# RWKV-style scan on one core: k, w and r in another channel order, v copied once a batch into its own tile, two working tiles instead of four

## The reference, cut to what matters

```python
xk, xw, xv, xr, xg = ...            # five learned mixes of x and x shifted by one position
w = exp(-exp(time_decay + tanh(xw @ td_w1) @ td_w2))   # (b, l, h, s), h = 32 heads, s = 16
r, k, v = xr @ Wr.T, xk @ Wk.T, xv @ Wv.T              # the same shape
def step(s, rkvw):                  # for each head a 16 x 16 state, s[i, j]
    a = k_t[..., :, None] * v_t[..., None, :]
    out = einsum('bhi,bhij->bhj', r_t, u * a + s)
    s = a + w_t[..., :, None] * s
    return s, out
out = scan(step, s0, (r, k, v, w))  # 128 steps
og = groupnorm(out) * gn_w + gn_b
x1 = x + og * silu(xg @ Wg.T) @ Wo.T
...                                 # a feed-forward part with three 512 x 512 products
...                                 # attention over ctx: scores, softmax, product, output
```

## Time and profile before

| | |
|---|---|
| median of 3 runs | 1021.33 us (1015.73, 1021.33, 1030.74) |
| profiled execution | 1016.36 us, its span 1014.6 us |
| busy: PE, DVE, POOL, ACT | 896.1, 691.5, 536.5, 396.5 us |
| mean granted TensorE clock | 0.936 of full |
| DMA | 150.69 MB, of which 64 v copies of 1 MB |
| first and last chunk | POOL starts at 112.8 us, PE has read the last at 777.6 us |

### The profile page before, as it was taken

How to read it: one execution, slowest core, us unless ns; L and a number is a source line. 1 busy time by engine, 2 the same in 40 slices (tenths; PEclk the granted TensorE clock), 3 DMA queues, 4 the chain that set the end, 5 groups by cost and what they waited for, 6 DMA issues and landing times.

```text
span 1014.6 us, 10745 instructions
## 1 busy us (share of the span) xinstructions
PE 896.1 (88%) x3588; PEld 398.5 (39%) x3588; DVE 691.5 (68%) x907; ACT 396.5 (39%) x819; POOL 536.5 (53%) x573
## 2 busy tenths in 40 slices
PE   1679978799786899688998999899998999979998
PEld 1233433343322343243343444344443454444454
DVE  6234499789988687888887698988998224442342
ACT  2013412333212241133223254565355554465395
POOL 2000388669987749648886778889682101000010
PEclk9687997899977899698999999999999999999999
DMA  7351679969689877878979844779642022001001
GB/s 270 134 125 73 179 178 222 233 171 233 162 187 216 209 184 196 212 145 224 243 182 281 216 112 100 183 192 227 163 99 83 21 73 83 21 4 39 21 0 42
DMA packets 100089, 150.69 MB, mean 149 GB/s; under 512 B 22850, under 2 KB 64066, under 8 KB 91842
## 3 DMA queue, kind: packets, MB, share of 16 engines
q1 hardware_dynamic: 73410, 129.03, 50.4%
q10 hardware_dynamic: 26624, 20.98, 8.5%
HBM read 115.38 MB, written 33.55 MB: 147 GB/s over the span
## 4 chain that ended last, share of the span: by engine, by line
PE 59%; DVE 14%; POOL 12%; issue 6%; ACT 5%; ACTq 2%; DMA 2%; SPq 0%; POOLq 0%; DVEq 0%
PE PS L1318 38%; PE PS L1381 4%; PE PS L1543 4%; POOL VB L704 4%; PE PS L1440 3%; PE PS L1520 2%; DVE PS L1033 2%; PE PS L1325 2%; POOL VB L699 2%; DVE VB L1150 2%; DVE M L1030 2%; DVE VB L1030 2%; POOL VB L695 2%; DVE M L1033 2%; PE PS L1454 1%
## 5 line engine op out<-in xcount | busy, mean ns | idle before, releaser
L1318 PE MATMUL PS<-M,W 128*128 128x512 f32 x672 | 329.8, 634 | 23.7 <-DVE M L1033 12.3
L1318 PEld LDWEIGHTS PS<-M,W 128*128 128x128 f32 x672 | 128.7, 202 | 198.2 <-issue 167.5
L704 POOL TENSOR_TENSOR VB<-VB 128x1024 f32<-128x1024 f32 x64 | 151.4, 2366 | 58.9 <-ACT VB L849 56.2
L1150 DVE TENSOR_TENSOR_SCAN VB<-PS,VB 128x512 f32<-128x512 f32 x128 | 149.1, 1206 | 25.9 <-POOL VB L704 17.3
L587 POOL TENSOR_SCALAR NM<-MV 128x2 f32<-128x2 f32 (+1 forms) x24 | 6.2, 258 | 283.7 <-DVE MV L1278 183.0
L1030 DVE TENSOR_TENSOR VB<-VB,PS 128x2048 f32<-128x2048 f32 x64 | 145.9, 2280 | 1.5
L695 POOL TENSOR_TENSOR VB<-KR,VB 128x1008 f32<-128x1008 f32 x64 | 129.7, 2026 | 17.5 <-DMA VB<-scr_vs 17.5
L699 POOL TENSOR_TENSOR VB<-WG,VB 128x1008 f32<-128x1008 f32 x64 | 129.3, 2020 | 0.0
L1033 DVE SCALAR_TENSOR_TENSOR PS<-PS,VEC,SX 128x512 f32<-128x512 f32 x80 | 60.2, 752 | 87.7 <-PE PS L1381 72.4
L1318 PE MATMUL PS<-W,M 128*128 128x512 f32 x224 | 105.1, 595 | 0.0
L1296 DVE TENSOR_REDUCE SM<-PS 128x1 f32<-128x512 f32 x64 | 44.0, 688 | 58.9 <-PE PS L1543 58.4
(11 more groups left out here) (167 smaller groups left out, 1280.5 us busy)
## 6 DMA issues: line engine op xcount, KB each, us to landing
VB<-scr_vs SPq DMA_DIRECT2D x64, 1024.0 KB, 7.9
W<-in_w SPq DMA_DIRECT2D x8, 1024.0 KB, 9.8
X<-in_x SPq DMA_DIRECT2D x4, 1024.0 KB, 8.2
scr_vs<-STG ACTq DMA_DIRECT2D x64, 64.0 KB, 5.7
scr_v<-STG ACTq DMA_DIRECT2D x16, 256.0 KB, 6.9
scr_w<-STG ACTq DMA_DIRECT2D x16, 256.0 KB, 8.3
scr_k<-STG ACTq DMA_DIRECT2D x16, 256.0 KB, 2.7
KR<-scr_k SPq DMA_DIRECT2D x16, 256.0 KB, 8.1
```

The source lines that it names most:

```text
L704: po.tensor_tensor(flat(bv[:, 0]), flat(bv[:, 0]), flat(bv[:, 1]), ALU.add).then_inc(g_kv, 1)
L1150: sc = dv.tensor_tensor_scan(s_, PS[:, 5, :], b_, 0.0, ALU.mult, ALU.add)
L1318: mm = pe.matmul(o, l, r, start=i == 0, stop=i == 3)
```

## The change

- **Order of k, w, r.** The host orders k, w, r, the decay, the initial state and `u` by `turn` like v: chunk m now has rows m, m+4, m+8 and m+12 of all 32 heads (partition = 32 x one of the four rows + head). HEAD is filled accordingly; its shape and the matmuls that use it stay.
- **One v copy a batch.** All four chunks of a batch need the same v layout now (32 heads, 4 times over), so v comes in by one copy of 1 MB per batch instead of four: 16 copies instead of 64.
- **Tiles.** VB keeps its four tiles. Two (2 and 3) hold v of a batch, in turn; two (0 and 1) are the working tiles of the chunks (`NB = 2`). The v copy waits for POOL's last operation on the batch two before (`g_kv`). POOL reads v there and writes the working tile, so that POOL's first product of chunk k waits for PE to have read chunk k-2.
- **Initial state.** ACT's copy of zeros is gone; POOL's add runs over columns 1 to 63 of 16 rows (1,008) and no longer waits for ACT; DVE's scan waits for the remaining ACT copy; ACT's copy waits for PE's chunk k-2.
- **Tables.** All five ORDER tables are new.

```diff
-NB = 4
+NB = 2
...
-    "a:23 l:1 a:1 l:1 a:2 p:2 a:1 p:11 a:1 p:3 a:5 p:1 a:1 p:1 a:1 p:3 a:1 p:16 a:1 p:4 a:1 p:9 a:11 p:1 "
+    "a:26 l:2 p:6 a:1 p:7 a:1 p:3 a:5 p:1 a:1 p:1 a:1 p:8 a:1 p:6 a:1 p:7 a:1 p:5 a:8 p:1 a:4 p:1 a:4 "
...
-        VB = sb("VB", [P, NB, 2, S, N2])
+        VB = sb("VB", [P, 4, 2, S, N2])
...
-                    for m in range(C4):
-                        k = C4 * bb + m
-                        if k >= NB:
-                            w.wait_ge(p_scan, k - NB + 1)
-                        for c in range(C4):
-                            w.wait_ge(d_vs[c], 64 * (q + 1))
-                        w.wait_ge(d_s0, 32)
-                        src = vs_rows[q, bb % QB, 8 * m:8 * m + 8].unsqueeze(0).to_broadcast([S, 8, S * L])
-                        sp.dma_start(VB[:, k % NB].rearrange("p s j n -> p (s j n)"), src).then_inc(d_vb[k % NB], 16)
-                        yield
-                        if m == 0:
...
+                    if bb >= 2:
+                        w.wait_ge(g_kv, 12 * (bb - 1))
+                    for c in range(C4):
+                        w.wait_ge(d_vs[c], 64 * (q + 1))
+                    w.wait_ge(d_s0, 32)
+                    src = vs_rows[q, bb % QB].unsqueeze(0).to_broadcast([4, H, S * L])
+                    sp.dma_start(VB[:, 2 + s].rearrange("p s j n -> p (s j n)"), src).then_inc(d_vb[s], 16)
+                    yield
...
-                    w.wait_ge(d_vb[k % NB], 16 * (k // NB + 1))
+                    w.wait_ge(d_vb[s], 16 * (bb // 2 + 1))
+                    if k >= NB:
+                        w.wait_ge(p_scan, k - NB + 1)
                     vo, ve = bv[:, 0, :, 1:N2], bv[:, 1, :, 1:N2]
-                    po.tensor_tensor(vo, KO[:, 0:N2 - 1].unsqueeze(1).to_broadcast([P, S, N2 - 1]), vo,
-                                     ALU.mult).then_inc(g_kv, 1)
+                    po.tensor_tensor(vo, KO[:, 0:N2 - 1].unsqueeze(1).to_broadcast([P, S, N2 - 1]),
+                                     VB[:, 2 + s, 0, :, 1:N2], ALU.mult).then_inc(g_kv, 1)
...
                     w.wait_ge(g_kv, 3 * k + 2)
-                    w.wait_ge(a_s0, 2 * k + 2)
-                    po.tensor_tensor(flat(bv[:, 0]), flat(bv[:, 0]), flat(bv[:, 1]), ALU.add).then_inc(g_kv, 1)
+                    po.tensor_tensor(vo, vo, ve, ALU.add).then_inc(g_kv, 1)
...
-                    w.wait_ge(d_vb[k % NB], 16 * (k // NB + 1))
+                    if k >= NB:
+                        w.wait_ge(p_scan, k - NB + 1)
                     w.wait_ge(v_hd, C4 + 2)
                     ac.activation(VB[:, k % NB, 0, :, 0], S0[:, k, :], ACT.Copy).then_inc(a_s0, 1)
-                    yield
-                    ac.activation(VB[:, k % NB, 1, :, 0], S0[:, k, :], ACT.Copy, scale=0.0).then_inc(a_s0, 1)
                     yield
...
                     w.wait_ge(g_kv, 3 * (k + 1))
+                    w.wait_ge(a_s0, k + 1)
...
-    w8 = [heads(p0("Wk")).T, turn(p0("Wv")).T, heads(p0("Wr")).T, turn(p0("Wg")).T, turn(p0("Wo").T)]
+    w8 = [turn(p0("Wk")).T, turn(p0("Wv")).T, turn(p0("Wr")).T, turn(p0("Wg")).T, turn(p0("Wo").T)]
```

More of the change, by code:

```diff
@@ L317, in rwkv_attention_kernel @@
         d_vs = [sem(f"d_vs{i}") for i in range(4)]
-        d_vb = [sem(f"d_vb{i}") for i in range(NB)]
+        d_vb = [sem(f"d_vb{i}") for i in range(2)]
         d_st_ = {n: [sem(f"d_scr_{n}{m}") for m in range(4)] for n in NAMES}
@@ L490, in stream_load @@
                     yield
-                    for m in range(C4):
-                        k = C4 * bb + m
-                        if k >= NB:
-                            w.wait_ge(p_scan, k - NB + 1)
-                        for c in range(C4):
-                            w.wait_ge(d_vs[c], 64 * (q + 1))
-                        w.wait_ge(d_s0, 32)
-                        src = vs_rows[q, bb % QB, 8 * m:8 * m + 8].unsqueeze(0).to_broadcast([S, 8, S * L])
-                        sp.dma_start(VB[:, k % NB].rearrange("p s j n -> p (s j n)"), src).then_inc(d_vb[k % NB], 16)
-                        yield
-                        if m == 0:
-                            for ready in stored("r", q):
-                                w.wait_ge(*ready)
-                            if bb >= 2:
-                                w.wait_ge(p_end, 3 * bb - 4)
-                            sp.dma_start(KR[:, s, 1], of_batch("r", bb)).then_inc(d_rg[s], 16)
-                            yield
+                    if bb >= 2:
[6 more added lines that the diff above has]
+                    yield
+                    for ready in stored("r", q):
+                        w.wait_ge(*ready)
+                    if bb >= 2:
+                        w.wait_ge(p_end, 3 * bb - 4)
+                    sp.dma_start(KR[:, s, 1], of_batch("r", bb)).then_inc(d_rg[s], 16)
+                    yield
                     for ready in stored("v", q):
@@ L692, in stream_scan @@
                         yield
-                    w.wait_ge(d_vb[k % NB], 16 * (k // NB + 1))
+                    w.wait_ge(d_vb[s], 16 * (bb // 2 + 1))
+                    if k >= NB:
+                        w.wait_ge(p_scan, k - NB + 1)
                     vo, ve = bv[:, 0, :, 1:N2], bv[:, 1, :, 1:N2]
-                    po.tensor_tensor(vo, KO[:, 0:N2 - 1].unsqueeze(1).to_broadcast([P, S, N2 - 1]), vo,
-                                     ALU.mult).then_inc(g_kv, 1)
+                    po.tensor_tensor(vo, KO[:, 0:N2 - 1].unsqueeze(1).to_broadcast([P, S, N2 - 1]),
+                                     VB[:, 2 + s, 0, :, 1:N2], ALU.mult).then_inc(g_kv, 1)
                     yield
                     w.wait_ge(g_wp, 2 * (bb + 1))
-                    po.tensor_tensor(ve, KE[:, 0:N2 - 1].unsqueeze(1).to_broadcast([P, S, N2 - 1]), ve,
-                                     ALU.mult).then_inc(g_kv, 1)
+                    po.tensor_tensor(ve, KE[:, 0:N2 - 1].unsqueeze(1).to_broadcast([P, S, N2 - 1]),
+                                     VB[:, 2 + s, 1, :, 1:N2], ALU.mult).then_inc(g_kv, 1)
                     yield
                     w.wait_ge(g_kv, 3 * k + 2)
-                    w.wait_ge(a_s0, 2 * k + 2)
-                    po.tensor_tensor(flat(bv[:, 0]), flat(bv[:, 0]), flat(bv[:, 1]), ALU.add).then_inc(g_kv, 1)
+                    po.tensor_tensor(vo, vo, ve, ALU.add).then_inc(g_kv, 1)
                     yield
@@ L1178, in stream_end @@
                     w.wait_ge(g_sel, 1)
-                    dv.tensor_reduce(HEAD[:, m, 0, 8 * m:8 * m + 8], ID[:].rearrange("p (i h) -> p h i", h=8), AX_X,
+                    dv.tensor_reduce(HEAD[:, m, 0], ID[:].rearrange("p (g h) -> p h g", h=H), AX_X,
                                      ALU.add).then_inc(v_hd, 1)
@@ L1588, in layout @@
     a = {k: np.asarray(v) for k, v in inp.items()}
-    heads = lambda w: w.reshape(C4, 8, S, -1).transpose(0, 2, 1, 3).reshape(E, -1)
     turn = lambda w: w.reshape(H, 4, 4, -1).transpose(2, 1, 0, 3).reshape(E, -1)
@@ L1602, in layout @@
     vec += [cols(p0("maa_stack")[0, f]) for f in MIXES]
-    vec += [cols(heads(p0("time_decay"))[:, 0])] + [cols(turn(p0(n))[:, 0]) for n in ("gn_w", "gn_b")]
+    vec += [cols(turn(p0("time_decay"))[:, 0])] + [cols(turn(p0(n))[:, 0]) for n in ("gn_w", "gn_b")]
     vec += [cols(p0(n)) for n in ("ln2_w", "ln2_b", "ffn_maa_k", "ffn_maa_r")]
@@ L1618, in layout @@
         "td1": chunks(p0("td_w1")),
-        "td2": np.concatenate([heads(p0("td_w2").T).T] * 2),
+        "td2": np.concatenate([turn(p0("td_w2").T).T] * 2),
         "wl1": np.stack([odd(p1("Wn").T), p1("Wm").T, p1("Wl"), odd(p1("Wo")).T], axis=1),
@@ L1622, in layout @@
         "st01": ctx[:, 0:2, :].reshape(B, 2, C4, P).transpose(3, 2, 1, 0),
-        "s0": ctx[:, 2:2 + S, :].reshape(B, C4, 8, S, S).transpose(3, 2, 0, 1, 4).reshape(P, B * C4, S),
-        "u": heads(p0("u").reshape(E)).reshape(C4, P).T,
+        "s0": ctx[:, 2:2 + S, :].reshape(B, H, 4, 4, S).transpose(2, 1, 0, 3, 4).reshape(P, B * C4, S),
+        "u": turn(p0("u").reshape(E)).reshape(C4, P).T,
     }
```

## The result

The changed kernel takes **1060.3 us** (median of 4, 1056.82 to 1064.16), the kernel before 1020.3 beside it: ratio **1.0378** [1.0289, 1.0467], slower. The forecast was 1009, its range ended at 1046, and "slower" had a chance of 0.22. The profiled execution took 1064.16 us, its span is 1062.4.

The account below looks back on a forecast made before the run. PE was nearly full everywhere, with the chunks at times setting the pace, 54 us at most. From 1016.4, -24 for POOL's waits and +12 for two tiles gave 1004 profiled; from 1021.3, 1009 us; range 978 to 1046.

Parts of the forecast that it names:

- slower: Whole kernel: the outcome beyond the measurable 2%, above 1042 us; chance 0.22.
- Hidden: SP queue: the v copy has about one batch, 41 us, against a landing of 7.9, so it costs 0.
- The landing of 7.9 us: v copies: time to landing, read from the trace before and used for the new copy, 7.9 us.
- four engines: Rival, v copies: a leading broadcast of 4 keeps each copy to four DMA engines, landing 31.6 us; 1047 us, chance 0.12.
- The rival's price, 38 us,: Four engines, v copies: 14 us for the first batch plus 24 for transfers SP issues behind a copy; 1009 to 1047.
- -24 us for POOL's waits: POOL beside the chunks: its waits for ACT and the copies, 73.7 us, go; -24 us, bounds 0 and -54.
- The share rule: POOL: 45% of what makes it late goes, so 45% of the chunks' 54 us is won, -24 us.
- +12 for two tiles: Working tiles: POOL's product of chunk k waits for PE's chunk k-2; +12 us, between 0 and 161.
- tiles decide: Rival, working tiles: chunks still taking 22.5 us make two tiles set the pace; 1062 us, chance 0.14.
- the 40 allowed: POOL: sign of a right forecast, a new wait for PE L1440 of under 40 us in all.
- 0 for the 48 copies that go: DMA beside the chunks: 48 copies of 1 MB fewer; 0 beside what is counted elsewhere, bound -20 us.
- 0 for the matmuls moved ahead: PE behind the last chunk: 28 matmuls fewer, 25 us, only cover for a later last chunk; 0.

Follow-up runs that it names:

- 16-engine version: The changed kernel with each batch's v copy issued as four transfers of 32 partitions, each over all 16 DMA engines: 992.5 us, ratio 0.9768 to the kernel before.
- The ACT part alone: The kernel before with only POOL's add over 1,008 columns without waiting for ACT, and ACT's zero copy gone: 1033.6 us, ratio 1.0171.
- the clash removed: The kernel before with POOL's add freed of ACT, plus two waits keeping POOL's products off DVE's M<-SX,VEC,EXT operations: 1018.5 us, ratio 0.9987.

## Why the prediction was wrong, point by point

- **"Hidden": 41 us of cover against a landing of 7.9.** This step failed, and both of its numbers were wrong. The 41 us were the pace of the chunks, as if SP issued the copy the moment its tile was free. SP's wait for PE was removed, but others took its place (L516 217.8 us, L510 173.7), and the copy stands behind them. The cover was 20 us in the median, so a landing of 19 to 24 us was late, and POOL waited for it at eight batches of 16. Of the two numbers the landing decided: the 16-engine version has no more cover and is 68 us faster. The tables with the queue's order were at hand; that the cover ends where the queue's own waits begin could be seen in them.
- **The landing of 7.9 us** was taken from a copy of another shape. Issued the new way it is 21.2 in the median. The chance of 0.12 for "four engines" was too small: the mechanism stood in a rule, the diff had exactly the shape, and nothing in the trace spoke against it. The Trainium skill, "DMA: Bandwidth & Descriptors", section "Rules for kernel authors", has the slowest dimension set the number of engines. Here the trace agrees: four late events a copy where there were sixteen, and 21.2 us with 4 in front for 7.9 with 16 in front, so 2.7 times, not four.
- **The rival's price, 38 us,** was too low against 68. Its first part (14 for the first batch) measured 4 at most. What was missed is that it strikes in later batches too, and about half of it strikes others: the load of r, the stores of g. The rival named LT<-LE as the victim; that one stayed at 2.0 us in the median, with one of 16 at 20.0.
- **-24 us for POOL's waits** failed as well. The ACT part alone brought +15, and 0 with the clash removed. The share rule (45% of 54 us) took a freed engine for a faster kernel. POOL's waits moved to the next one in its order.
- **+12 for two tiles.** A third tile gained nothing, so there is no sign of this cost; all four were not tried. The mean time of a chunk, from its first product to its last matmul, came out at 19.7 us for the forecast 18.9: the working was sound, and "tiles decide" didn't happen, though POOL's wait for PE (77.9) was twice the 40 allowed. The wait was slack.
- **0 for the 48 copies that go:** right for their bytes, to 0.2%.
- **0 for the matmuls moved ahead** was the other failure, with the opposite sign. 25 us were counted as cover for late chunks, and no more. But PE bounds the stretch behind the last chunk (busy 195 of 203 us, before 224 of 237), so work that leaves it is time won if the chunks keep their pace: 34 us there, of which 15 went in later chunks. With the copy repaired the change is worth 24 us (1016.5 to 992.5), more than the forecast's 12. PE's idle time in 161:778 is 45.1 us there, before 60.7, which fits with more work beside the chunks. So the table speaks for the order and not for POOL's waits; but the order by itself was not run, and this stays argued.

## What to carry to other kernels

Before counting the bytes of a transfer, look at its first dimension: a copy of 1 MB with 4 in front took 21.2 us where one with 16 in front took 7.9, and it delayed loads and stores issued behind it. Read a transfer's cover from the issuing queue's order and waits, not from when its tile comes free. And when an engine is freed, look at what it will run beside: an operation that comes earlier can land on a neighbour that it slows.

## What the hardware showed that was not expected

**DVE and POOL hinder each other in some pairs.** M<-SX,VEC,EXT (two operands in SBUF) takes 0.75 us alone and 2.4 to 2.8 where POOL's product or add runs beside all of it, and the product then takes 2.45 for 2.00. DVE's product VB<-VB,PS, with one operand in PSUM, took 2.25 to 2.29 us wherever it stood, and the scans 1.2. The Trainium skill, "SBUF — State Buffer", section "SBUF: two separate sides", describes a port pair that DVE and GpSimd share, an exclusive lock which a DVE operation with two SBUF inputs contends for against a GpSimd operation that reads SBUF, and which goes to whichever starts first. The traces agree with that in whom it strikes, and two waits gave back 15 us in one kernel and 11 in another. At 381 us in the kernel before it is POOL that loses: small operations of it took 1.22 and 1.11 us, for 0.24 and 0.25, beside DVE's SX<-EXT, which had come first there, and 0.57 to 0.66 beside the four M<-SX,VEC,EXT, which kept their 2.74 us:

```profile
380.38 2.79 DVE L1030 TENSOR_TENSOR SX<-EXT 128x1024 f32<-128x1024 f32 x2
383.21 2.74 DVE L1033 SCALAR_TENSOR_TENSOR M<-SX,VEC,EXT 128x512 f32<-128x512 f32 x4
```

```profile
380.87 1.22 POOL L607 TENSOR_TENSOR GT<-GR 128x32 f32<-128x32 f32 x1
```

**A short idle time of PE is paid for again behind it.** In the kernel with POOL's add freed, PE stood idle for 6.6 us at 392 us. The granted clock was 0.50 in the 3.5 us behind that, which is the lower of its two levels (1.2 and 2.4 GHz), and 0.75 in the next 7.0. PE's next three rows took 10.6 us, for 7.2 in the kernel before. The last of them has twelve instructions, 7.11 us for 5.37 in the earlier trace rows:

```profile
402.05 7.11 PE L1317 MATMUL PS<-M,W 128*128 128x512 f32 x12
```
